# Attention scores as one-pass products of high and low parts, with the maxima subtracted in a product of their own

## The chip, the cores and the metric

One NeuronCore of a Trainium2 chip runs the whole program. The metric is the device time of one execution, in microseconds (us). Engines are named as in the profile: PE (TensorE) with its weight loads PEld, DVE (VectorE), ACT (ScalarE), POOL (GpSimd), SP (SyncE, which issues the DMAs).

## The reference

Input x is 8 batches of 512 tokens by 256 numbers, f32. Four layers follow, each on a layer norm of x, with its result added to x:

- layer 0, causal attention: 16 heads of 16 numbers, queries and keys rotated (RoPE), scores divided by 4, masked above the diagonal, softmax, values, output weights;
- layers 1 and 3, gated attention: a sigmoid gate picks the 256 best of the 512 tokens; among them attention with 16 heads of 16 numbers, without mask; the result is multiplied by the gate and put back at the tokens' places;
- layer 2, biased attention: 16 heads of 64 numbers, with a table of relative biases added to the scores.

```python
scores = jnp.einsum('bhnd,bhmd->bhnm', Q, K) / jnp.sqrt(jnp.asarray(d_k, x.dtype))
scores = jnp.where(causal, scores, -jnp.inf)
attn = jax.nn.softmax(scores, axis=-1)
out = jnp.einsum('bhnm,bhmd->bhnd', attn, V)
```

## The kernel before

All data stays in SBUF. The program is a list of steps (`Step(kind, s, l, n, q)`: kind, batch, layer, number), `c_*` for the causal layers, `f_*` for the gated and `b_*` for the biased ones. A batch's layers depend on each other, so layers of several batches run interleaved: from the third batch on, the order is a cycle in which the biased layer of one batch is mixed with the last gated layer of the batch before it and the causal and first gated layer of the next batch. `in_order` makes one order of all steps from a table of turns (`PLACE`), a table of durations (`WORK`) and dependencies; every engine runs its part of that order, and semaphores counted by `Plan` connect them. PSUM has eight banks, which `in_order` gives out too. Where PE would wait for over 1 us by that plan, L1341 has it transpose the identity.

**A causal layer.** `c_ln` and `c_xt` normalise and transpose x. `c_q` and `c_k` (n = 0, 1; 8 heads each) project; DVE turns pairs (L1159, L1160) and POOL finishes the rotation (L999, L1001). A group of 32 rows then holds two heads, 16 rows each. `c_hq` (ACT, L1051, L1052) makes two copies of the queries: in each, one head's rows are scaled by 1/4 and the other's are zero. `c_hk` (DVE, L1165, L1166) makes two copies of the keys, with the other head's rows zero and one of them minus one.

`c_p1` computes scores with queries as weights, four heads side by side in the four groups of 32 rows of PE, each into its own bank (L1379). DVE takes the row maxima (L1176, for a gated layer L1251) into `mcol`. `c_m` transposes `mcol` on PE (L1389), and DVE adds the maxima into the free rows of the queries (L1184), where they meet the key row of minus one. `c_p2` computes the scores again, transposed and with the maxima subtracted (L1399); ACT takes the exponential (L1057); POOL zeroes what lies above the diagonal (L1007). `c_va` and `c_vb` multiply by the values (L1413), beside which a column of ones gives the sums; DVE divides (L1195 to L1206). `c_y` applies the output weights. The steps come in three parts, since key tile t meets only queries from tile t on: products are 128 to 512 columns wide.

**A gated layer** does the same with 256 tokens (two tiles, products of 256 columns): `f_q` (ACT, L1062) and `f_k` (DVE, L1240) make the copies right out of PSUM, `f_p1` is L1469, `f_m` L1479, `f_p2` L1488. It also gathers and spreads tokens by products whose operands are F32R (a float that PE takes in one pass), split into a high and a low part (L1033, L993, L1072, L1282).

Every other product has f32 operands; each shows as two records in the trace.

## Time and profile before

| | us |
|---|---|
| median of 3 runs | 2102.8 (2101.93 to 2104.2) |
| profiled execution, its time | 2105.06 |
| its span | 2103.3 |
| busy: PE | 2029.9 (97%) |
| PEld | 1243.3 (59%) |
| DVE | 1467.4 (70%) |
| ACT | 1110.2 (53%) |
| POOL | 600.8 (29%) |

The span is the time from the first to the last instruction. Busy time of PE counts its matmul records with modelled ends, records that overlap once. The DMAs move 98.56 MB, 47 GB/s in the mean.

### The profile page before, as it was taken

Reading aid. Unit: us, or ns where it says so; the run is one execution under the profiler, and the core shown is the slowest. Engines: PE = TensorE matmul, PEld = TensorE weight load, DVE = VectorE, ACT = ScalarE, POOL = GpSimd, SP = SyncE. Lnnn points to the kernel's source line nnn. Section 1 sums busy time; section 2 is a strip of 40 time slices with the busy share of each in tenths; the row PEclk is TensorE's granted clock in tenths of the full one; section 3 lists DMA queues with packets and bytes.
Section 4 is the critical chain, followed back from the end, with each engine's and each line's share of the span. In section 5 each row is a group of like instructions: output and inputs, shape, how many; then the busy total and the mean of one; then the engine's idle time right before and its main releaser. Section 6 shows DMA issues by size and latency. Waiting matters only on the chain.

```text
span 2103.3 us, 38722 instructions
## 1 busy us (share of the span) xinstructions
PE 2029.9 (97%) x14644; PEld 1243.3 (59%) x14644; DVE 1467.4 (70%) x4578; ACT 1110.2 (53%) x2497; POOL 600.8 (29%) x817
## 2 busy tenths in 40 slices
PE   7889999999999999999999999999999999999997
PEld 4456556655665555765566645666456654666565
DVE  8887654777757766678767687576875777866435
ACT  1444664746537474464734646365563656535642
POOL 4212132243222342233411423124231243212220
PEclk9999999999999999999999999999999999999998
DMA  3001121121111110111101111012100121111200
GB/s 143 2 1 41 43 76 58 50 81 34 44 41 57 57 44 26 48 67 48 42 21 58 58 47 44 18 59 71 46 31 27 51 73 49 44 34 51 76 3 11
DMA packets 29047, 98.56 MB, mean 47 GB/s; under 512 B 2880, under 2 KB 11200, under 8 KB 28736
## 3 DMA queue, kind: packets, MB, share of 16 engines
q1 hardware_dynamic: 28864, 96.09, 13.6%
q8 instruction: 118, 1.93, 0.4%
q14 instruction: 65, 0.53, 0.1%
HBM read 91.89 MB, written 4.19 MB: 46 GB/s over the span
## 4 chain that ended last, share of the span: by engine, by line
PE 85%; DVE 7%; ACT 6%; issue 1%; POOL 0%; DMA 0%; SPq 0%; DVEq 0%; ACTq 0%; POOLq 0%
PE ps L861 26%; PE ps L1532 11%; PE ps L1550 10%; PE ps L1322 9%; PE ps L1540 9%; PE ps L1379 4%; PE ps L1488 3%; PE ps L1399 3%; PE ps L1500 3%; PE ps L1469 3%; PE ps L1413 2%; ACT PTc L1057 2%; ACT PT L1097 2%; DVE ps L1176 2%; DVE mcol L1251 1%; ACT probs L1088 1%
## 5 line engine op out<-in xcount | busy, mean ns | idle before, releaser
L1015 POOL TENSOR_SCALAR probs<-probs,rtotal 128x512 f32<-128x512 f32 x512 | 344.9, 693 | 871.8 <-DVE rtotal L1277 871.3
L1088 ACT ACTIVATE probs<-probs,peak 128x512 f32<-128x512 f32 x512 | 365.0, 714 | 220.9 <-DVE peak L1273 220.9
L1268 DVE CUSTOM_DVE_ANT_0 probs<-ps,band 128x512 f32<-128x512 f32 x512 | 332.6, 687 | 107.8 <-PE ps L1532 106.4
L1097 ACT ACTIVATE PT<-ps 128x512 f32<-128x512 f32 x512 | 263.1, 619 | 78.1 <-PE ps L1540 77.9
L1176 DVE CUSTOM_DVE_ANT_0 ps<-ps,later 128x128 f32<-128x128 f32 (+3 forms) x512 | 233.3, 525 | 40.9 <-PE ps L1379 40.0
L1540 PEld LDWEIGHTS ps<-ident,probs 128*128 128x128 f32 x2048 | 223.3, 141 | 52.0 <-issue 43.3
L1532 PE MATMUL ps<-KT,QT 64*128 64x512 f32 x1024 | 252.4, 611 | 0.0
L1540 PE MATMUL ps<-ident,probs 128*128 128x128 f32 x2048 | 248.3, 275 | 0.1
L1550 PE MATMUL ps<-PT,Vb 128*64 128x512 f32 x1024 | 235.9, 600 | 0.1
L861 PE MATMUL ps<-xnT,wb 128*128 128x512 f32 x512 | 233.0, 598 | 1.3 <-ACT PT L1097 0.7
L1057 ACT ACTIVATE PTc<-ps 128x384 f32<-128x384 f32 (+1 forms) x384 | 167.7, 542 | 64.8 <-PE ps L1399 64.7
L1251 DVE TENSOR_REDUCE mcol<-ps 128x2 f32<-128x512 f32 x256 | 157.3, 683 | 14.8 <-PE ps L1469 14.0
L1068 ACT ACTIVATE PTf<-ps 128x512 f32<-128x512 f32 x256 | 131.7, 604 | 63.0 <-PE ps L1488 62.6
L861 PEld LDWEIGHTS ps<-xnT,wb 128*128 128x128 f32 x512 | 92.9, 190 | 102.0 <-issue 96.8
L1532 PEld LDWEIGHTS ps<-KT,QT 64*128 64x128 f32 x1024 | 94.5, 186 | 92.9 <-issue 67.9
L1550 PEld LDWEIGHTS ps<-PT,Vb 128*64 128x64 f32 x1024 | 67.1, 137 | 139.2 <-issue 121.8
L861 PEld LDWEIGHTS ps<-wb,xnT 128*128 128x128 f32 x1024 | 122.6, 192 | 26.5 <-issue 16.7
L1007 POOL TENSOR_SCALAR_AFFINE_SELECT PTc<-PTc 128x512 f32<-128x512 f32 x128 | 82.1, 654 | 178.0 <-ACT PTc L1057 177.3
L983 POOL TENSOR_TENSOR rstd<-veps,pow_half 128x2 f32<-128x2 f32 x64 | 47.0, 737 | 280.8 <-DVE veps L1118 280.8
L861 PE MATMUL ps<-wb,xnT 128*128 128x128 f32 x1024 | 125.7, 276 | 0.0
L1322 PE MATMUL ps<-wob,OTb 128*128 128x256 f32 x512 | 114.0, 380 | 0.8 <-DVE OTb L1279 0.8
L1379 PE MATMUL ps<-K,Qz 32*128 32x128 f32 (+3 forms) x1024 | 96.5, 471 | 14.8 <-ACT PTc L1057 4.9
(133 smaller groups left out, 2887.3 us busy)
## 6 DMA issues: line engine op xcount, KB each, us to landing
band<-in_band SPq DMA_DIRECT2D x64, 896.0 KB, 4.6
wb<-in_w_b SPq DMA_DIRECT2D x64, 384.0 KB, 3.0
x<-in_x SPq DMA_DIRECT2D x16, 256.0 KB, 2.9
out<-x SPq DMA_DIRECT2D x16, 256.0 KB, 2.2
wob<-in_wo_b SPq DMA_DIRECT2D x1, 1024.0 KB, 8.7
wqk<-in_wqk_a SPq DMA_DIRECT2D x1, 512.0 KB, 6.2
cos_t<-in_cos SPq DMA_DIRECT2D x1, 256.0 KB, 5.4
sin_t<-in_sin SPq DMA_DIRECT2D x1, 256.0 KB, 6.5
```

The lines of the kernel that those rows point to most:

```text
L861: last = nc.tensor.matmul(o, w, r, start=(i == 0), stop=(i == len(pairs) - 1))
L1015: last = g.tensor_scalar(unit, unit, rtotal[:, r % 8, e:e + 1], 1.0, ALU.mult, ALU.mult)
L1057: a.activation(pt_c(m, q)[:, h], bank(now, name)[:, 0:w], ACT.Exp).then_inc(act_read, 1)
L1088: last = a.activation(unit, unit, ACT.Exp, bias=peak[:, r % 8, e:e + 1], accum_out=total[:, r % 8, e:e + 1])
L1097: a.activation(PT[:, k % 2, e, :, tile_of(q)], bank(now, name).rearrange("p (k n) -> p k n", k=NT), ACT.Copy).then_inc(act_read, 1)
L1176: last = v.tensor_tensor_reduce(out=scores, in0=scores, in1=later[:, NT * P - w:NT * P], scale=1.0, scalar=-3e38, op0=ALU.add, op1=ALU.max ...
L1268: v.tensor_tensor_reduce(out=probs[:, r % ROWS_HELD, e, :], in0=bank(now, name), in1=band[:, k % 2, e, lo:lo + T], scale=1.0, scalar=-3e38 ...
L1322: last = te.matmul(o[:, j * D:(j + 1) * D], w, r, start=(k == 0 and j == 0), stop=(k == count - 1 and j == 1))
L1379: last = te.matmul(o[h][:, at_:at_ + w], m.Qz[group(h), c, e, tile_of(t)], m.K1[group(h), c, e, 0:w], start=True, stop=True)
L1532: full(te.matmul(bank(now, name), QT2[half(e), k % 2, tile_of(q)], KT2[half(e), k % 2, :], start=True, stop=True), now, name)
L1540: last = te.transpose(bank(now, name)[:, tile_of(t)], probs[:, r % ROWS_HELD, e, tile_of(t)], ident[:])
L1550: last = te.matmul(o[half(e), :], Vb[:, k % 3, q, half(e)], PT[:, k % 2, e, q, :], start=(q == 0), stop=(q == NT - 1))
```

## The change

Queries and keys of the causal and gated layers are stored as F32R. A head's 16 numbers are copied to all 32 rows of a group, and X holds the high part of the queries in 16 rows and the rest (the low part) in the other 16. HI holds the high part of the keys in both halves, LO the rest in both. X by HI plus X by LO is then the full product. The first score product is these two, the second these two and a third one, in which a selecting weight `sel` (0 and -1) picks the high and low part of the maxima from M. The factor 1/4 moves into the exponential.

New steps: `c_dq`, `c_dk` (DVE: two shuffles each that copy one head's rows to both halves), `c_rq`, `f_rq` (ACT: X = plus or minus the copy, rounded), `c_xq`, `f_xq` (DVE: X = copy in the low half + X), `c_hk`, `f_hk` (ACT: HI; POOL: LO = copy - HI), `c_hm`, `f_hm` (DVE: high and low part of the maxima, in small pieces). `c_m` and `f_m` are read out by ACT instead of DVE. `f_q` and `f_k` become two shuffles each from PSUM. The values lie closer together (17 columns a head instead of 32), the work memory of the layers is laid out anew, and both tables `PLACE` and `WORK` are new, so the order of all steps is another.

```diff
     for i in range(2):
-        out += [(c("q", i), [c("xt")], []), (c("k", i), [c("xt")], []), (c("hq", i), [c("q", i)], []),
-                (c("hk", i), [c("k", i)], [])]
+        out += [(c("q", i), [c("xt")], []), (c("k", i), [c("xt")], []), (c("dq", i), [c("q", i)], []),
+                (c("rq", i), [c("dq", i)], []), (c("xq", i), [c("rq", i)], []), (c("dk", i), [c("k", i)], []),
+                (c("hk", i), [c("dk", i)], [])]
...
+                        if kind in ("c_hk", "f_hk"):
+                            for e in range(2):
+                                pool.wait_ge(high_k_done, plan.after("high_k", now, now) - 1 + e)
...
+                                last = g.tensor_tensor(low, both, high, ALU.subtract)
+                            last.then_inc(halves_k_done, 1)
...
+                            act.wait_ge(pairs_q_done, plan.after("pairs_q", Step("c_dq", s, l, n), now))
+                            for e in range(2):
+                                last = a.activation(m.X[:, n, e], m.Dq[:, n, e], ACT.Copy, scale=sides[:, 0:1])
+                            last.then_inc(signed_done, 1)
+                        if kind in ("c_m", "f_m"):
+                            parts = m.M[n][:] if kind == "c_m" else m.M[:, n]
+                            a.activation(parts, bank(now) if kind == "c_m" else bank(now)[:, 0:CAP],
                                          ACT.Copy).then_inc(act_read, 1)
...
                         if kind == "c_p2":
                             _, w = c_p2_parts(q)
+                            if n == 0 and q == 0:
+                                act.wait_ge(halves_q_done, plan.after("halves_q", Step("c_xq", s, l, 1), now))
...
+                                a.activation(pt_c(m, q)[:, h], bank(now, name)[:, 0:w], ACT.Exp,
+                                             scale=float(DH) ** -0.5).then_inc(act_read, 1)
...
+                            for e in range(2):
+                                last = v.stream_shuffle(pairs[:, n, e], turned, [DH * e + r % DH for r in range(32)])
+                            last.then_inc(done, 1)
+                        if kind in ("c_xq", "f_xq"):
...
+                                last = v.scalar_tensor_tensor(out=parts, in0=both, scalar=sides[:, 1:2], in1=parts,
+                                                              op0=ALU.mult, op1=ALU.add)
...
+                            v.tensor_copy(split[:, :, :, 0:2], top[:, :, :, 4:6]).then_inc(high_m_done, 1)
+                            dve.wait_ge(high_m_done, plan.after("high_m", now, now))
+                            v.tensor_tensor(split[:, :, :, 2:4], top[:, :, :, 4:6], split[:, :, :, 0:2],
+                                            ALU.subtract).then_inc(halves_m_done, 1)
...
                             for t, at_, w in parts:
-                                for h in range(4):
-                                    last = te.matmul(o[h][:, at_:at_ + w], m.Qz[group(h), c, e, tile_of(t)],
-                                                     m.K1[group(h), c, e, 0:w], start=True, stop=True)
...
+                                for some in (m.LO, m.HI):
+                                    for h in range(4):
+                                        last = te.matmul(o[h][:, at_:at_ + w], m.X[group(h), c, e, tile_of(t)],
+                                                         some[group(h), c, e, 0:w], start=(some is m.LO), stop=(some is m.HI))
...
                             for t, at_, w in parts:
-                                for h in range(4):
-                                    last = te.matmul(o[h][:, at_:at_ + w], m.K1[group(h), c, e, tile_of(t)],
-                                                     m.Qz[group(h), c, e, t * P:T], start=True, stop=True)
...
+                                for i in range(3):
+                                    for h in range(4):
+                                        one = sel[group(h), e:e + 1].to_broadcast([32, P])
+                                        w_ = (m.LO[group(h), c, e, tile_of(t)], m.HI[group(h), c, e, tile_of(t)], one)[i]
+                                        r_ = m.M[c][group(h), t * P:T] if i == 2 else m.X[group(h), c, e, t * P:T]
+                                        last = te.matmul(o[h][:, at_:at_ + w], w_, r_, start=(i == 0), stop=(i == 2))
```

## Rows read from the trace of the kernel before

**Rows 1.** Busy time by stretch: us, then PE, PEld, DVE, ACT, POOL, clock, DMA.

```profile
0.00:160.00 160.00, 132.40 (x1125) 74.94 (x1125) 132.83 (x422) 59.47 (x125) 49.78 (x69) 0.96 0.13 48
160.00:2045.00 1885.00, 1854.82 (x13145) 1135.33 (x13142) 1301.55 (x4075) 1038.89 (x2350) 547.75 (x745) 1.00 0.14 48
2045.00:2103.30 58.30, 42.65 (x380) 33.04 (x378) 33.06 (x81) 11.87 (x23) 3.31 (x3) 0.91 0.03 10
```

**Rows 2.** The same of one period, the second of five alike.

```profile
840.00:1093.00 253.00, 248.87 (x1806) 151.09 (x1806) 182.35 (x572) 138.90 (x312) 74.54 (x100) 1.00 0.14 47
```

**Rows 3.** Records of one line by stretch: L1379 (first row), then L1469; PE, PEld.

```profile
0.00:160.00 160.00, 25.65 (x256) 10.59 (x256) 0.96 0.13 48
...
0.00:160.00 160.00, 4.30 (x64) 3.09 (x64) 0.96 0.13 48
2045.00:2103.00 58.00, 4.30 (x64) 3.09 (x64) 0.91 0.03 10
```

**Rows 4.** Groups by line: busy us, mean ns, idle before and releasers.

```profile
L1469 PE MATMUL ps<-K1f,Qzf 32*128 32x256 f32 x1024 | 72.5, 398 | 9.9 <-DVE mcol L1251 3.0 <-DVE peak L1268 1.8 <-ACT Qzf L1062 1.7
```

**Rows 5.** Timeline of PE, last gated layer: start, us, line, form, count.

```profile
2071.72 2.01 PE L1469 MATMUL ps<-K1f,Qzf 32*128 32x256 f32 x32 [0.59 <-ACT Qzf L1062]
2075.51 1.15 PE L1469 MATMUL ps<-K1f,Qzf 32*128 32x256 f32 x16 [1.78 <-DVE mcol L1251]
```

**Rows 6.** Timeline of PE, causal layers (the first row holds 128 and 256 columns).

```profile
477.67 0.94 PE L1379 MATMUL ps<-K,Qz 32*128 32x128 f32 x16
...
50.97 0.93 PE L1379 MATMUL ps<-K,Qz 32*128 32x384 f32 x8 [0.86 <-DVE mcol L1176]
52.30 1.14 PE L1379 MATMUL ps<-K,Qz 32*128 32x512 f32 x8 [0.41 <-ACT PTc L1057]
```

**Rows 7.** Timeline of PE, one-pass products; two of another tile lie between.

```profile
2098.15 0.40 PE L1322 MATMUL ps<-of_hi,spread_t 128*128 128x256 f32 x2
...
2098.63 0.40 PE L1322 MATMUL ps<-of_hi,spread_t 128*128 128x256 f32 x2
```

**Rows 8.** Groups by line of DVE.

```profile
L1159 DVE STREAM_SHUFFLE Qz<-ps 128x512 f32<-128x512 f32 x16 | 11.8, 735 | 0.0
L1206 DVE STREAM_TRANSPOSE Qz<-Qz 128x512 f32<-128x512 f32 x16 | 11.4, 711 | 0.5
L1165 DVE TENSOR_SCALAR K<-K,sides 128x512 f32<-128x512 f32 x16 | 11.3, 708 | 0.4 <-POOL K L1001 0.4
L1166 DVE TENSOR_SCALAR K<-K,sides 128x512 f32<-128x512 f32 x16 | 15.3, 953 | 0.0
L1184 DVE SCALAR_TENSOR_TENSOR Qz<-ps,sides,Qz 128x512 f32<-128x512 f32 x32 | 22.4, 741 | 0.9 <-PE ps L1389 0.9
L1184 DVE SCALAR_TENSOR_TENSOR Qzf<-ps,sides,Qzf 128x256 f32<-128x256 f32 x64 | 28.0, 478 | 23.1 <-PE ps L1479 23.1
L1240 DVE TENSOR_SCALAR K1f<-ps,sides 128x512 f32<-128x512 f32 x32 | 24.4, 804 | 11.4 <-PE ps L861 11.4
L1273 DVE TENSOR_SCALAR peak<-peak 128x2 f32<-128x2 f32 x256 | 49.9, 195 | 8.9
```

**Rows 9.** Groups by line of ACT and POOL.

```profile
L1072 ACT ACTIVATE of_hi<-ps 128x512 fp32r<-128x512 f32 x16 | 9.6, 597 | 56.6 <-PE ps L1322 56.6
L993 POOL TENSOR_TENSOR xn_lo<-xn,xn_hi 128x512 fp32r<-128x512 f32 x32 | 40.1, 1275 | 62.1 <-ACT xn_hi L1033 62.1
```

**Rows 10.** One line's instructions: duration ns min/median/max.

```profile
L1201 DVE TENSOR_TENSOR scaledf<-turnedf,rsums x64: 291/292/749, 154.9 to 2093.3; 128x128 f32<-128x128 f32 x64
```

**Rows 11.** Timeline, first score product and last gated layer's queries.

```profile
25.31 1.67 PE L1379 MATMUL ps<-K,Qz 32*128 32x128 f32 x16 [3.95 <-ACT Qz L1052]
...
2070.40 1.26 ACT L1062 ACTIVATE Qzf<-ps,sides 128x512 f32<-128x512 f32 x2 [5.82 <-PE ps L861]
```

**Rows 12.** Timeline of PE, products of one column; four lie between the two.

```profile
111.11 0.16 PE L861 MATMUL ps<-ones,tie 128*128 128x1 bf16 x1
...
111.23 0.16 PE L861 MATMUL ps<-ones,tie 128*128 128x1 bf16 x1
```

718 lines of the change are left out of this document (407 added, 311 removed).

## The prediction

> **What bounds the kernel now.** I read the busy time by stretch first, then one cycle, then the timeline at both ends.
> TensorE (PE) is busy for 1854.8 of the 1885 us between 160 and 2045 us [rows 1], at the full clock: this is the bound. That part is a pattern of 253.1 us, repeated; in one period PE is idle for 4.1 of 253 us, while VectorE (DVE) is busy for 182 us, 72% [rows 2]. A microsecond of PE work taken out there shortens the span, as long as DVE keeps up.
> The ends are different. In the first 160 us PE is idle for 27.6 us and DVE is busy for 132.8 us, 83%: a chain through all engines, with DVE nearest to the bound. In the last 58.3 us PE is idle for 15.7 us [rows 1].
> The changed products are a small part of PE's time. Two of the eight causal layers have their first score products in the first 160 us (256 of 1024 records); one of the sixteen gated layers has its own there, one in the last 58 us (64 each of 1024) [rows 3]. So 6 causal and 14 gated layers lie where PE is the bound.
>
> **What a score product costs now.** An f32 product is two records (1024 records for 512 products of L1469) [rows 4]. Four heads sit in four groups of 32 rows and run side by side; I call four such records a batch. 32 records of 256 columns take 2.01 us and 16 take 1.15 [rows 5]: 0.86 us for four batches, 0.215 each. The step with two batches of 128 and two of 256 columns takes 0.94 [rows 6], 0.21 less than four of 256, so 128 columns cost 0.1075 a batch. 512 against 384 columns is 1.14 against 0.93 for two batches [rows 6], again 0.105 per 128 columns. So a batch takes 0.43, 0.3225, 0.215 and 0.1075 us for 512, 384, 256 and 128 columns, in proportion, weights included.
>
> **What one costs after.** The operands become one-pass floats (F32R): queries X (high part in 16 rows, low part in the other 16), keys HI and LO. The first product needs two records (X by LO, X by HI), as many as now. The second needs three: the third subtracts the maxima. The trace has one-pass products of 256 columns: four start within 0.48 us, 0.12 each [rows 7]. That is 0.0125 more than half of 0.215, so something besides the columns counts, most likely the load of the weights. I take 0.12 for 256 columns and half of today's price for 384 and 512 (0.161, 0.215). For 128 columns nothing is shown: at least 0.054 (half of today's), at most 0.215 (four passes, twice today's); I take 0.12, the nearest one-pass row.
> Per four heads of a causal layer, each width counted once: now 1.075 times 2 = 2.15 us in either product; after, 0.616 times 2 = 1.23 in the first and times 3 = 1.85 in the second. It saves 0.92 and 0.30, times 4 per layer 4.88 us. Gated, two tiles of 256: 0.86 now, 4 x 0.12 = 0.48 and 6 x 0.12 = 0.72 after; 0.52 times 4 = 2.08 us per layer. All layers: 8 x 4.88 + 16 x 2.08 = 72.3 us. Where PE is the bound: 6 x 4.88 + 14 x 2.08 = 58.4 us.
> The Trainium skill ("TensorE: Matmul & The Clock Gate", section "LDWEIGHTS (loading the stationary operand)") gives columns / 1.2 GHz for a weight load, whatever the rows: 107 ns for 128 columns. By it the load would set the pace of narrow products and speak against splitting them: 128-column batches gain nothing and the third one is pure loss. With 0.107 for both 128 and 256 columns the 72.3 would be 84.8. The trace fits it as far as it goes: f32 at 128 columns shows 0.1075, which two passes explain as well.
> The four transposes of the maxima per step stay (two in a gated layer).
>
> **What the other engines get.** DVE loses, per causal layer, L1165 and L1166 (2 x (0.708 + 0.953)) and four of L1184 at 0.741: 6.3 us. It gains eight shuffles, at 0.735 as from PSUM (the transposes of L1206, SBUF to SBUF, take 0.711, so the source matters little), four X updates with two SBUF inputs at 0.741, and four tiny splits of the maxima at 0.195: 9.6. Net +3.3. Per gated layer it loses 2 x 0.804 + 4 x 0.478 = 3.5 and gains 4 x 0.735 + 2 x 0.741 + 4 x 0.195 = 5.2, net +1.7 [rows 8]. In all +54 us on 1467, +6.7 us in a cycle.
> ScalarE (ACT) gains, per causal layer, four high copies (0.6) and two copies of the maxima (0.6); its four scaled copies stay: +3.6. Gated: +2.4 at most. GpSimd (POOL) gains four, or two, subtractions of 1.275 us: 82 us in all [rows 9]. Both have room in a cycle (139 and 75 of 253 us [rows 2]); other work of PE, the biased layer, hides them. DMAs don't change; the queues are passed by no new transfer.
> New waits: ACT, at the first exponentials of a causal layer, waits for the second half of X; behind it stand copies for the biased layer. The work memory overlaps more closely too, so some steps get a fixed order. I price these in the idle time.
> DVE seems to be held up now and then already: L1201, which reads two SBUF tensors, takes 0.292 us in the median and 0.749 at most [rows 10]. The Trainium skill ("SBUF — State Buffer", section "SBUF: two separate sides") has an exclusive lock on a port pair: a DVE operation with two SBUF inputs and a GpSimd one block each other for a whole instruction. The 64 new X updates and 48 subtractions of maxima are of that kind. By it, with POOL busy for a third of the time, a third of the 112 would wait for half a POOL instruction (0.64), 24 us of DVE time and one point of its share, which the bounds of the idle time hold.
>
> **Idle time in the middle.** It can stay at 4.1 us in a cycle (bound below), or follow DVE's share (bound above): 72% with 1.6% idle in a cycle, 83% with 17% in the first stretch. After the change DVE has 189 of some 245 us, 77%. The first stretch is one chain with little to fill it in, the middle has the biased layer, so I stay near the lower end: 1 us more a cycle, over 7.4 cycles 7 us.
>
> **The ends.** At the start PE waits for ACT's scaled copy of the queries until 25.31 [rows 11]. The way from the rotated query to the product is two ACT copies, 1.26 us if they are as those of L1062 [rows 11]; it becomes two shuffles (1.47), two copies and two updates (1.48), 4.2. The keys' way becomes two shuffles, a copy and two POOL subtractions, 4.6 instead of the 1.7 of L1165 and L1166 [rows 8, 9]. That is 3 us until the first product, and 3 again in the first gated layer, whose queries and keys go the same ways. Together +6. Faster products don't give this back while DVE works on the maxima. Bounds: -14 (all of PE's savings there count), +16 (DVE's extra 10 us come on top of the 6).
> At the end the same 3 before the first product of the last gated layer (at 2071.72 [rows 5]), and -0.5 for earlier maxima and a shorter way through them: +2.5. The exponentials on ACT set the pace there, not PE.
>
> **Sum.** -58.4 + 7 + 6 + 2.5 = -42.9 us. The profiled execution took 2105.06 us (span 2103.3 and 1.8 around it), 2.3 above the median of 2102.8. So 2062, or 2060 as a median.
>
> **Rivals.**
> A, everything counts: the new order hides the ends and the idle time stays. -72.3, 2030; if narrow batches cost half of today's, another 20 less (160 of 128 columns by 0.066, 800 of 256 by 0.0125), 2010. For it: five like cycles with 4 us idle show how well the order can fit. Against it: 83% DVE in the first 160 us. 0.20.
> B, 128 columns take four passes: 160 batches (64 in the first, 96 in the second products) times 0.095, 15 us more: 2075. No row for or against. 0.14.
> C, DVE becomes the bound, on the slower side. Place: the waits of PE for banks of score tiles that DVE reads the maxima from, in the middle. If the idle time follows DVE's share to 9%, half way between the two stretches, it is 23 us a cycle, 19 more, 141 in all instead of 7: 2194. At half that growth, which I hold for more likely, it is 70 instead of 7: 2123, the time I give it. It decides from 7 us more a cycle on, where the 42.9 are used up. Against it: in the middle DVE's work is independent of PE's next step most of the time. 0.09, a part of which ends near no change.
> D, records can't be issued this fast. A batch of four in 0.107 us is 27 ns a record; the fastest stream shown is five records in 0.12 us [rows 12], 24 ns, but with weights of another type. At 50 ns a batch takes 0.2; 960 narrow batches times 0.08, and 6 for those of 384 columns, are 83 more: 2143. Break-even near 41 ns. 0.06.
> My forecast, between 2040 and 2074: 0.51.
>
> **How the numbers follow.** 2060 is the likeliest. 2018 to 2094 takes in A's 2030 but not its outer end, and B; it leaves out C and D. A difference of 0.2% (4 us) is what can be told from none. Slower takes most of C and D, 0.10; within 0.2% 0.04; faster 0.86.
>
> **What would show it.** One-pass batches of four heads 0.12 us apart, 0.16 and 0.215 for the wide ones; if those of 128 columns are 0.2 apart, it is B, if all are near 0.2, D. A cycle of about 245 us with some 5 us of PE idle; 250 or more, with PE waiting for DVE, is C. The first score product after 28 us, biased layers starting some 6 us later. DVE near 1520 us, POOL near 680. I am wrong if PE's busy time falls by less than 60 us or if its idle time, 73 us now, grows by more than 30.

## The result and the profile after

The changed kernel takes 2115.5 us (median; 2111.4 to 2120.6), the kernel before in the same job 2103.2. The ratio is 1.0056, 95% interval 1.0037 to 1.0075: it is slower by half a per cent, where 2060 was forecast. The profiled execution took 2120.6 us, its span is 2117.8. It is the slowest of the five and 5 us above their median; the clock (below) is most of the difference.

Busy time by stretch of the changed kernel; columns as in [rows 1], and behind them one of its periods, as in [rows 2]:

```profile
0.00:160.00 160.00, 121.11 (x1045) 80.84 (x1049) 133.04 (x447) 51.82 (x108) 56.65 (x69) 0.79 0.13 48
160.00:2045.00 1885.00, 1810.76 (x14154) 1135.66 (x14148) 1377.37 (x4288) 1097.29 (x2476) 629.61 (x804) 0.99 0.15 48
2045.00:2117.80 72.80, 56.35 (x503) 47.40 (x501) 39.22 (x100) 14.55 (x28) 6.53 (x6) 0.90 0.05 15
...
1110.00:1363.20 253.20, 242.21 (x1935) 152.43 (x1934) 193.30 (x604) 145.37 (x326) 86.41 (x108) 0.99 0.14 47
```

The period has hardly changed: 253.2 us in this one, 253.5 in the mean of six, where the kernel before has 252.7. TensorE's busy time in it fell from 248.9 to 242.2, and its idle time rose from 4.1 to 11.0. DVE does 193.3 us of work in place of 182.3; 189 had been forecast.

Where the time went by place. As marks I take the first product with the output weights (`wob`) in the first and in the last biased layer, that is near the layer's end. In the kernel after they start as follows (timeline of PE: start, us, line, form, count); in the kernel before they start at 338.20 and 2032.66 us:

```profile
350.81 0.63 PE L1440 MATMUL ps<-wob,OTb 128*128 128x256 f32 x2
...
2044.87 0.59 PE L1440 MATMUL ps<-wob,OTb 128*128 128x256 f32 x2
```

So the start, up to that first mark, costs 12.6 us. What lies between the marks gives back 0.4 (1694.1 for 1694.5): six periods are longer by 0.8 each, and the shorter stretch behind them takes 173.3 in place of 178.3. What follows 2044.87 takes 72.9 in place of 70.6, 2.3 more. The sum is the 14.5 us between the spans.

The products themselves came out as forecast. The last gated layer once more, as in [rows 5], now by batches of four records:

```profile
2085.02 0.29 PE L1593 MATMUL ps<-gHI,gX 32*128 32x256 f32 x4
2085.14 0.29 PE L1593 MATMUL ps<-gLO,gX 32*128 32x256 f32 x4
2085.25 0.29 PE L1593 MATMUL ps<-gHI,gX 32*128 32x256 f32 x4
2085.37 0.29 PE L1593 MATMUL ps<-gLO,gX 32*128 32x256 f32 x4
...
2088.55 0.45 PE L1593 MATMUL ps<-gHI,gX 32*128 32x256 f32 x4
2088.77 0.45 PE L1593 MATMUL ps<-gLO,gX 32*128 32x256 f32 x4
```

At the full clock a batch starts 0.12 us behind the last, as in [rows 7]; the last two rows show 0.22 for the same batch at half clock. At the full clock, within a run of such batches, the next one mostly comes 0.058 to 0.116 us behind one of 128 columns, 0.12 behind 256, 0.17 behind 384 and 0.22 to 0.23 behind 512. Behind the first batch of a run the trace has some 0.07 more (0.13 to 0.17 for 128 columns).

What PE waits for between 160 and 2045 us, in its four largest groups (us in total, times, longest):

```profile
PE ps L1498 <- DVE X L1279: 12.8, 12, 1.9
PE ps L943 <- DVE above L1344: 8.4, 6, 1.4
PE ps L1522 <- DVE peaks L1295: 7.9, 6, 1.3
PE ps L1593 <- DVE peaks L1369: 7.0, 12, 0.9
```

In the kernel before PE's largest wait there is for ACT's exponentials (6.2 us), and the largest for DVE is 3.7. The first row is the wait for the new update of the queries; the two with `peaks` are waits for banks from which DVE has yet to take the maxima. One such place, DVE's timeline first, then GpSimd's, then PE's (start, us, line, form, count, and in brackets the idle time before it and its releaser):

```profile
968.89 0.76 DVE L1272 STREAM_SHUFFLE Dq<-Xf 128x512 f32<-128x512 f32 x1
969.54 3.35 DVE L1279 SCALAR_TENSOR_TENSOR X<-Dq,sides,X 128x512 fp32r<-128x512 f32 x2
...
968.18 2.50 POOL L1087 TENSOR_TENSOR LO<-LOf,HI 128x512 fp32r<-128x512 f32 x2
970.63 1.71 POOL L1077 TENSOR_TENSOR HIf<-HIf,sin_t 128x512 f32<-128x512 f32 x1
...
972.95 0.33 PE L1498 MATMUL ps<-LO,X 32*128 32x128 f32 x4 [1.93 <-DVE X L1279]
```

and the same two instructions 32 us later, with no GpSimd work beside them:

```profile
1001.73 1.41 DVE L1279 SCALAR_TENSOR_TENSOR X<-Dq,sides,X 128x512 fp32r<-128x512 f32 x2
```

3.35 against 1.41 us, 1.94 more, and PE is idle for 1.93 at that place. The first update starts 0.1 us into the second GpSimd subtraction and ends 0.5 us behind it, the second waits out the rotation's product; the shuffle above, which reads one SBUF tensor, keeps its 0.76 beside the same GpSimd instruction. The groups (ns min/median/max):

```profile
L1279 DVE SCALAR_TENSOR_TENSOR X<-Dq,sides,X x32: 742/1096/1840, 22.7 to 1764.0; 128x512 fp32r<-128x512 f32 x32
L1279 DVE SCALAR_TENSOR_TENSOR gX<-gDq,sides,gX x32: 743/1060/1822, 143.0 to 2084.0; 128x512 fp32r<-128x512 f32 x32
L1272 DVE STREAM_SHUFFLE Dq<-Xf x32: 735/750/779, 18.8 to 1730.6; 128x512 f32<-128x512 f32 x32
```

The eight updates of a period take 9.6 us; at 0.74 they would take 5.9. Behind the idle time the clock goes down too (window rows as above; the seventh figure is the granted clock):

```profile
966.00:973.70 7.70, 5.78 (x29) 2.52 (x28) 7.03 (x13) 2.58 (x5) 7.54 (x6) 1.00 0.00 0
973.70:977.20 3.50, 3.50 (x14) 2.14 (x16) 2.93 (x17) 1.19 (x2) 0.33 (x1) 0.53 0.02 5
```

PE had been idle for 1.9 us, then ran 3.4 us at 1.2 in place of 2.4 GHz. There are eight such drops between 160 and 2045 us, and none in the kernel before, whose longest gap there is 1.03 us. Four come behind this wait for X (1.9 us), four behind the wait for the maxima at L1522 (1.3 us); each of the two waits comes six times at the same length, and two times without a drop. A third wait, of 1.4 us, comes six times and has none behind it. So a gap of this length can cost a drop and need not. A period with one drop lasts 253.3 us, one with two 254.9: 1.6 us each, 13 in all. The number differs between executions: the mean clock is 0.974 in the profiled one and 0.979 in the two fastest, which take 9 us less. By my estimate (0.005 of 2115 us, lost at half speed) that is 21 us less at half clock and some 10 us of time, so most of the difference between executions is the clock, and the median execution likely has fewer than eight drops.

### The profile page after: what moved, and what is told of

Read it like the earlier page. It is cut to its first block, busy times and chain, and to the rows that moved or that the text cites. A ratio compares the mean times of both kernels' runs of the same rounds, so it can differ in the third digit from the quotient of the medians.

```text
span 2117.8 us, 41412 instructions
## 1 busy us (share of the span) xinstructions
PE 1988.2 (94%) x15696; PEld 1263.9 (60%) x15696; DVE 1549.6 (73%) x4835; ACT 1163.7 (55%) x2610; POOL 692.8 (33%) x879
## 4 chain that ended last, share of the span: by engine, by line
PE 70%; DVE 18%; ACT 6%; POOL 3%; issue 2%; DMA 0%; SPq 0%; DVEq 0%; POOLq 0%
PE ps L943 17%; PE ps L1678 10%; PE ps L1660 10%; PE ps L1440 9%; PE ps L1668 7%; DVE ps L1295 3%; ACT PTc L1166 3%; PE ps L1522 3%; PE ps L1536 3%; PE ps L1627 3%; PE ps L1498 2%; DVE peaks L1369 2%; DVE probs L1386 2%; PE ps L1615 2%; PE ps L1593 2%
## 5 line engine op out<-in xcount | busy, mean ns | idle before, releaser
L1102 POOL TENSOR_SCALAR probs<-probs,rtotal 128x512 f32<-128x512 f32 x512 | 352.3, 708 | 549.5 <-DVE rtotal L1395 549.2
L1202 ACT ACTIVATE PT<-ps 128x512 f32<-128x512 f32 x512 | 264.5, 610 | 71.2 <-PE ps L1668 70.6
L1295 DVE CUSTOM_DVE_ANT_0 ps<-ps,later 128x512 f32<-128x512 f32 (+3 forms) x512 | 232.9, 525 | 32.1 <-PE ps L1498 31.9
L1668 PE MATMUL ps<-ident,probs 128*128 128x128 f32 x2048 | 254.3, 277 | 0.5
L1166 ACT ACTIVATE PTc<-ps 128x384 f32<-128x384 f32 (+1 forms) x384 | 167.1, 545 | 42.4 <-PE ps L1522 41.5
L1369 DVE TENSOR_REDUCE peaks<-ps 128x2 f32<-128x512 f32 x256 | 157.3, 682 | 14.0 <-PE ps L1593 13.9
L943 PE MATMUL ps<-wb,xnT 128*128 128x128 f32 x1024 | 132.3, 285 | 0.0
L1440 PEld LDWEIGHTS ps<-wob,OTb 128*128 128x128 f32 x512 | 96.4, 190 | 12.6
```

The costliest lines, as they stand in the source:

```text
L943: last = nc.tensor.matmul(o, w, r, start=(i == 0), stop=(i == len(pairs) - 1))
L1102: last = g.tensor_scalar(unit, unit, rtotal[:, r % 8, e:e + 1], 1.0, ALU.mult, ALU.mult)
L1166: a.activation(pt_c(m, q)[:, h], bank(now, name)[:, 0:w], ACT.Exp, scale=float(DH) ** -0.5).then_inc(act_read, 1)
L1202: a.activation(PT[:, k % 2, e, :, tile_of(q)], bank(now, name).rearrange("p (k n) -> p k n", k=NT), ACT.Copy).then_inc(act_read, 1)
L1295: last = v.tensor_tensor_reduce(out=scores, in0=scores, in1=later[:, NT * P - w:NT * P], scale=1.0, scalar=-3e38, op0=ALU.add, op1=ALU.max ...
L1369: v.tensor_reduce(places[:, h:h + 1].rearrange("p h t -> p (h t)"), bank(now, name).rearrange("p (t n) -> p t n", t=NS), AXIS.X, ALU.max). ...
```

## The experiments

The runs came in five jobs, in which the kernel before has medians of 2103.8 to 2105.4 us. Each ratio is against the kernel before of its own job; differences between jobs are taken from the ratios (0.01 is 21 us) and are good to 3 to 5 us, by the intervals of the two ratios. Periods are read from the profiled execution alone; a mean of six is taken between the marks of the first seven biased layers. Line numbers are those of each run's own kernel.

**TensorE's part alone.** Before, with one-pass products in the number that the change has. Low parts are left out, the products of each kind being repeated instead.

```
-    last = te.matmul(o[h][...], m.Qz[...], m.K1[...], start=True, stop=True)      # f32
+    for again in range(2):                                                        # 3 in c_p2, f_p2
+        for h in range(4): last = te.matmul(o[h][...], m.QR[...], m.KR[...], ...)  # F32R
```

> The kernel before with its own order and its own side work; only the score products are one-pass records, as many as in the change (each product issued twice in the first, three times in the second score product, each time over the same bank). Left out: the low parts, so the scores are rounded. Theory S (the side work and the longer ways eat what PE saves): the whole gain of PE shows here, 2040 to 2055 us, a cycle of about 244 us. Theory K (one-pass products leave PE too idle and its clock falls to half, mostly in the first 160 us): the middle gains, but the first 160 us show 50 us or more at the half clock and the time is 2060 to 2075. If PE's time is worth nothing in this schedule at all: 2095 or more.

2072.2 us, ratio 0.9852 (0.9837 to 0.9868): 32 us, not 58 to 72. A period of it:

```profile
1079.80:1328.00 248.20, 240.88 (x1935) 151.59 (x1934) 181.99 (x572) 138.59 (x312) 74.27 (x100) 1.00 0.15 48
```

PE works 8.0 us less in a period ([rows 2] has 248.9 in 253.0), and the period is 4.8 shorter; the rest, 3.2 us, has become idle time, with DVE's work unchanged. The time lies in theory K's range, but only 24 us before 160 us are at half clock, where K wanted 50 or more. Theory S had 2040 to 2055 and a period of 244, so it doesn't hold in full either: a part of the gain is missing without any new side work.

**The rest of the change alone.** The changed kernel, each score product one f32 product of X by HI (the low part of the keys and the product with the maxima are left out of the scores, all side work is kept).

```
-    for some in (m.LO, m.HI):  ... te.matmul(o[h][...], m.X[...], some[...], start=(some is m.LO), ...)
+    for some in (m.HI,):       ... te.matmul(o[h][...], m.X[...].bitcast(F32), some[...].bitcast(F32), start=True, ...)
```

> The changed kernel, its order and side work unchanged, but each score product is one f32 product of X by HI (two records, as before the change), so PE has the cost of the kernel before. Left out: LO, the maxima in the second product. Theory S (PE is no longer the bound): it costs little, 2110 to 2135 us. If PE's saving still counts in full in the changed kernel: 2175. Theory K: the clock stays up in the first 160 us, and the start is shorter than in the changed kernel by some 8 us although PE has more work.

2156.5 us, ratio 1.0257 (1.0234 to 1.0280): the side work and the new order cost 52 us when TensorE saves nothing. Theory S had 2110 to 2135, and 2175 stood for a saving that counts in full; the changed kernel is 42 us below this run, so TensorE's saving is worth 42 us in it.

```profile
1125.70:1385.60 259.90, 250.90 (x1807) 151.61 (x1806) 194.63 (x604) 145.97 (x326) 86.65 (x108) 0.99 0.14 46
```

6.6 us in a full period (6.3 in the mean of six), and 12 until the first mark (350.2): the whole loss of the start is in this part.

**Is it the new order?** The changed kernel under the turn table of before (steps that it lacks placed at those they split from).

```
-    PLACE = { ... }   # the new table
+    PLACE = { ... }   # that of the kernel before
```

> The changed kernel under the table of turns of the kernel before: the common steps have their old turns, a new step the turn of the step it stems from (c_dq, c_rq, c_xq that of c_hq; c_dk, c_hk that of c_hk; c_hm that of c_m; f_rq, f_xq that of f_q; f_hk that of f_k; f_hm that of f_m). Theory O (the new order is what lost the gain): 2050 to 2085 us. Theory S: 2110 to 2140, since the old turns know nothing of the side work.

2364.6 us, ratio 1.1241 (1.1224 to 1.1259), a period of 286.7; both theories had expected less than 2140. So the old table isn't the better one for this work: the new order hides most of what the side work would cost in the old one. The planner saw the waits too: PE transposes the identity 1230 times in this run and 272 times in the changed kernel. What the new order costs by itself, with the side work of before, no run shows.

**Is it the clock at the start?** Dummy one-pass batches in the causal layers of the first two sequences, two in the first score product (shown) and one in the second.

```
+    for _ in range(2 if s < 2 else 0):
+        for h in range(4): te.matmul(o[h][...], m.X[...], m.HI[...], start=True, stop=True)
```

> The changed kernel, but in the causal layers of the first two batches PE issues more one-pass records over the same banks, four instead of two in the first and four instead of three in the second product, which is what the f32 products cost. The result is the same. Theory K: the time at the half clock in the first 160 us falls from 75 us to under 30, and the start is shorter by 5 to 12 us: 2103 to 2110 us. Theory S: PE waits there for DVE anyway, 2114 to 2120.

2122.4 us, ratio 1.0093 (1.0073 to 1.0113). The time at half clock before 160 us fell from 68 to 34 us, and the first mark came at 350.9, for 350.8 in the changed kernel. PE has more work there and a faster clock, and the start is the same to 0.1 us: it waits for other engines, unless the two cancel. The whole is 7 to 8 us slower than the changed kernel's median, but this profiled execution has eight drops between 160 and 2045 us and takes 2121.0, like the changed kernel's profiled one.

**What is TensorE's time still worth?** As the first run, each product once.

```
-    for again in range(2):
+    for again in range(1):
```

> The kernel before with each score product one one-pass product (no second or third pass over the bank; the low parts of queries and keys are left out), its order and side work unchanged. Against the run with two and three passes (2072.2) it takes away 32 batches of four records at 0.12 or less in every cycle of the scores of one causal and two gated layers, some 5 to 6 us of TensorE a cycle by the 0.118 measured for a batch behind 256 columns. Theory A (TensorE is still the bound in before's side work, what it saves is mostly given back): 3 to 5 us a cycle less, 2035 to 2050. Theory B (with its order kept, the kernel is already at the limit of VectorE and the waits, so that TensorE's time no longer counts): under 1.5 us a cycle, 2062 to 2072.

2049.3 us, ratio 0.9738 (0.9724 to 0.9753), 24 us less again. PE has some 11 us less to do in a period (I had written 5 to 6), and the period falls from 248.3 to 245.2, the mean of six: less than a third of TensorE's time is paid back. A part goes to the clock: between 160 and 2045 us 48 us are at half clock, 17 in the first run.

**Taking the update of the queries out** (and with it their low part); PE, and ACT before the first exponentials of a causal layer, wait for ACT's rounded copy.

```
-    if kind in ("c_xq", "f_xq"): ... v.scalar_tensor_tensor(out=parts, in0=both, ...)
-    at_least(pe, halves_q_done, ...)
+    at_least(pe, signed_done, ...)
```

> The changed kernel without the second step on the queries (VectorE's multiply-add of 0.72 us, 8 in a cycle = 5.8 us, about 56 in all), TensorE waits for ScalarE's rounded copy in its place; the low part of the queries is left out, order and everything else kept. Theory V (VectorE's added work, and its place at the end of the queries' chain, makes TensorE wait): the waits for X (12.8 us in the middle, 12 of them) go and some of the others shorten, 3 to 5 us a cycle, 2075 to 2095. Theory O (the new order, found for costs of its own, is what takes the time; waits only change their names): within 1 us a cycle, 2108 to 2118. Theory K (the keys' chain over ScalarE and GpSimd is as late as the queries'): the same as O here, and the next run moves.

2081.6 us, ratio 0.9886 (0.9869 to 0.9902): 36 us below the changed kernel and some 5 a period, as theory V had it. The first mark comes at 343.2, 7.6 us sooner.

**The update moved to ACT and GpSimd**, same result:

```
+    a.activation(m.Dq[...], m.Dq[...], ACT.Copy, scale=sides[:, 1:2]).then_inc(signed_done, 1)
-    last = v.scalar_tensor_tensor(out=parts, in0=both, scalar=sides[:, 1:2], in1=parts, ...)
+    last = g.tensor_tensor(parts, both, parts, ALU.add)
```

> The changed kernel with the same result, the second step on the queries moved off VectorE: ScalarE scales the pairs (0.65 us, 8 more in a cycle) and GpSimd adds them (1.3 us, 8 in a cycle). VectorE has 5.8 us a cycle less, the queries' chain is some 2.5 us longer from the shuffle to the last write where it has no queue to stand in. Theory V by occupancy (VectorE's time counts wherever it falls): 2085 to 2105. Theory V by latency (only the end of the queries' chain counts): slower than the changed kernel by up to 2.5 us at each of 24 causal and gated layers, 2120 to 2160. Theory O: 2110 to 2125.

2213.3 us, ratio 1.0513 (1.0492 to 1.0534). DVE is busy for 186.6 us a period instead of 193.3, and the period is 266. PE now waits for GpSimd:

```profile
PE ps L1591 <- POOL gX L1084: 45.1, 12, 5.6
PE ps L1496 <- POOL X L1084: 28.5, 6, 4.8
```

It is slower than the 2120 to 2160 expected of the longer way alone, and 113 us of its middle are at half clock. How late X is counts, wherever it is made.

**GpSimd's low part of the keys left out**; PE takes the rounded keys twice.

```
-    if kind in ("c_hk", "f_hk"): ... last = g.tensor_tensor(low, both, high, ALU.subtract)
-    for some in (m.LO, m.HI):
+    for some in (m.HI, m.HI):
```

> The changed kernel without GpSimd's low part of the keys (1.4 us each, 8 in a cycle); TensorE takes the rounded keys twice, so the number of its products is kept; order and the rest kept. The low part of the keys is left out. The keys' chain is 2.8 us shorter. Theory K: 3 us a cycle or more and an earlier first score product, under 2100. Theories V and O: within 1 us a cycle in the middle, 2105 to 2118; at the start the first score product may come up to 2.8 us earlier.

2095.1 us, ratio 0.9953 (0.9938 to 0.9968): 22 us below the changed kernel. In part it isn't the keys that come earlier, but the updates of the queries that are no longer held up:

```profile
L1270 DVE SCALAR_TENSOR_TENSOR X<-Dq,sides,X x32: 737/745/1832, 22.5 to 1741.7; 128x512 fp32r<-128x512 f32 x32
```

The median is 745 ns, against 1096 with GpSimd's subtractions beside it.

**Handing on by half.** Same work, order and result; signals for each of the two halves.

```
+    dve.wait_ge(signed_done, plan.after("signed", ..., now) - 1 + e)      # inside the loop over e
-    at_least(pe, halves_q_done, plan.after("halves_q", Step("c_xq", s, l, c), now))
+    at_least(pe, halves_q_done, plan.after("halves_q", Step("c_xq", s, l, c), now) - 1 + e)   # keys alike
```

> The changed kernel, same work, same order, same result, but its two preparation chains are handed on by half (head e=0 or 1) and not by pair: VectorE's second step on half 0 starts when ScalarE has rounded half 0, and TensorE's first score product of a pair waits for half 0 alone (of the keys' low part too; in gated layers ScalarE also starts behind the first shuffle). The queries' chain to the first product is some 1.2 to 2 us shorter, the keys' 1.4. Theory L (the time from projection to score product is paid nearly whole, since the order is fixed and holds no more work between: without the queries' second step, 1.44 us shorter, a cycle took 249 in place of 254): 4 to 6 us a cycle less, 2070 to 2092. Theory V (what counts is how long VectorE is occupied): no more than 1 us a cycle, 2108 to 2118.

2104.1 us, ratio 0.9992 (0.9980 to 1.0005): 13 us of the loss come back. That is between the theories: 2.7 us a period, where L wanted 4 to 6 and V no more than 1. Not all of it is latency: the eight updates of a period take 8.9 us in place of 9.6, and the middle of this profiled execution (2097.5 us, of the faster ones) has three drops, not eight. The first mark comes at 342.4, 8.4 us sooner.

**The update kept, but with PE not waiting for it** (ACT still does, before the first exponentials of a causal layer).

```
-    last = v.scalar_tensor_tensor(out=parts, in0=both, ...)      # PE: halves_q_done
+    last = v.scalar_tensor_tensor(out=both, in0=both, ...)       # PE: signed_done
```

> The changed kernel with the queries' second step still run by VectorE at its place in the order, but into a place that no score product reads: TensorE waits for ScalarE's rounded copy, as in the run without that step. The low part of the queries is left out of the scores. Theory L (its latency counts, VectorE's 5.8 us a cycle don't): 2080 to 2088, as without it (2081.6). Theory V: most of the 35 us comes back, 2100 to 2117.

2105.3 us, ratio 1.0005 (0.9995 to 1.0015). The ratio was 0.9886 without the update, is 1.0005 with it, and 1.0056 with PE's wait too: some 25 us go with DVE's occupied time (ACT's remaining wait is in them), 11 with PE's wait. Theory L, which I favoured by then, falls as the main cause.

**Both cuts together.**

```
-    if kind in ("c_xq", "f_xq"): ...
-    if kind in ("c_hk", "f_hk"): ... g.tensor_tensor(low, both, high, ALU.subtract)
```

> The changed kernel without the queries' second step and without GpSimd's low part of the keys, products and order kept (both low parts are left out). Theory L: the two savings don't overlap where one chain waits for the other, so more than either alone: a cycle of 244 to 247, 2050 to 2070. If the two cuts together give no more than the queries' alone (2078 to 2084), the rest of the loss is the order's or that of the other edits.

2078.4 us, ratio 0.9875 (0.9861 to 0.9890). That is 2 us below the first cut alone, which can't be told from none: the keys' subtractions cost mostly through the queries' updates. It is still some 5 above the first experiment, with the shuffles, the splits and the new order left.

**The keys' low part on DVE**, on top of the version by halves, same result.

```
-    pool.wait_ge(high_k_done, ...);  last = g.tensor_tensor(low, both, high, ALU.subtract)
+    dve.wait_ge(high_k_done, ...);   v.tensor_tensor(low, both, high, ALU.subtract)
```

> As the version that hands on by halves, and the low part of the keys is subtracted by VectorE (some 0.7 us each) and not by GpSimd (1.4 us): the keys' chain is 1.4 us shorter still, and VectorE has 8 x 0.7 = 5.6 us a cycle more to do. Same result. Theory L: the same as by halves or up to 2 us a cycle faster, 2060 to 2090. Theory V: 3 to 5 us a cycle slower than by halves.

2148.9 us, ratio 1.0211 (1.0179 to 1.0243), 45 us above the version by halves, though the keys' way is shorter.

```profile
DVE gLO L1280 <- ACT gHI L1149: 10.2, 13, 0.8
...
L1280 DVE TENSOR_TENSOR LO<-LOf,HI x32: 678/693/1751, 28.1 to 1778.0; 128x512 fp32r<-128x512 f32 x32
L1280 DVE TENSOR_TENSOR gLO<-gLOf,gHI x32: 683/692/693, 138.1 to 2108.9; 128x512 fp32r<-128x512 f32 x32
```

8 x 0.69 us a period and a wait at the head of DVE's queue, in which it stands still for what is behind it; the longest periods go from 252.0 to 259.4, more than the 3 to 5 us that theory V wanted.

**DVE's time by itself.** The kernel before, and seven idle shuffles of 256 columns behind the keys of every causal pair and gated layer, 28 a period.

```
+    for again in range(7):
+        if spent[0]: dve.wait_ge(spare_done, spent[0])
+        v.stream_shuffle(spare[:], cos_t[:, 0:256], [r ^ 1 for r in range(32)]).then_inc(spare_done, 1)
```

> The kernel before with idle work on VectorE, and nothing else: behind the preparation of the keys of every causal pair and of every gated layer seven shuffles of 256 columns (some 0.4 us each) into a place that nobody reads, 28 in a cycle, 11 to 12 us, what the change added there (182.3 to 193.3 us). No wait and no order is changed, and a shuffle is not held up by GpSimd. Theory S (before has slack: VectorE at 72% can take it): under 2 us a cycle, up to 2120. Theory V (in a fixed order VectorE's time at this place is nearly all on TensorE's path, as the run with the low part of the keys on VectorE showed with 45 us for 6): 6 to 11 us a cycle, 2150 to 2190.

2187.2 us, ratio 1.0392 (1.0376 to 1.0407), 82.5 us more. Its window row and one of its groups:

```profile
1145.60:1410.80 265.20, 253.77 (x1807) 153.45 (x1806) 194.24 (x628) 139.15 (x312) 74.84 (x100) 0.98 0.13 45
...
L1174 DVE STREAM_SHUFFLE spare<-cos_t x112: 432/436/446, 23.4 to 1798.9; 128x256 f32<-128x256 f32 x112
```

This experiment shows that DVE had little time to spare at this place. 28 x 0.436 = 12.2 us of work on an engine that is 72% busy, with no new wait between engines and no change of order, make the period 11.0 us longer (263.7 against 252.7, means of six): 0.9 us for each microsecond of DVE. (Each shuffle waits for the one before it, so seven take 3.31 us from start to end, for 3.06 of work.) In the period shown PE's idle time is 11.4 us in place of 4.1, and its busy time is up by 4.7 with the same products; it holds 10.2 us at half clock, as much as three drops, and at 1.6 us each they are that. So 0.6 of the 0.9 are waits, the rest is the clock. It is the price in an order that wasn't made for this work. In the changed kernel's order, made for its side work, the second experiment has 12 us more of DVE in a period (194.6 for 182.3) and a period 6.3 longer: 0.5 for one, with what ACT and GpSimd add in it.

**The same with two SBUF operands.**

```
-    v.stream_shuffle(spare[:], cos_t[:, 0:256], ...)
+    v.tensor_tensor(spare[:], cos_t[:, 0:256], sin_t[:, 0:256], ALU.mult)
```

> As the run before this, but the seven instructions at each place are products of two SBUF tensors of 256 columns (some 0.3 to 0.35 us each alone). Theory P: where GpSimd is busy each waits for it in addition, and GpSimd for it, so that they cost more per nominal microsecond than the shuffles do; in total near or above the shuffles in spite of a nominal time that is a quarter less. Theory V': three quarters of what the shuffles cost.

2210.1 us, ratio 1.0503 (1.0484 to 1.0522), 23 us more than the shuffles.

```profile
L1174 DVE TENSOR_TENSOR spare<-cos_t,sin_t x112: 417/425/1498, 23.9 to 1812.0; 128x256 f32<-128x256 f32 x112
L1255 DVE TENSOR_TENSOR spare<-cos_t,sin_t x112: 414/424/808, 137.3 to 2174.1; 128x256 f32<-128x256 f32 x112
```

Alone such an instruction takes 0.42 us, the shuffle's 0.44; the quarter less that I expected isn't there. But up to 1.50 beside GpSimd, which the shuffle never shows: 29 of the 224 take over 0.5 us, and all together they take 114.4 us for the shuffles' 97.9.

**Fewer turns.** The changed kernel, the two updates of a step as one instruction of 1024 columns; same work, order and result.

```
-    for e in range(2): ... v.scalar_tensor_tensor(out=m.X[:, n, e], in0=m.Dq[:, n, e], ...)      # 128x512
+    v.scalar_tensor_tensor(out=parts, in0=both, ...)      # m.X[:, n] and m.Dq[:, n], both e: 128x1024
```

> The changed kernel with the queries' second step as one instruction of 1024 columns in place of two of 512; the same work, order and result. In the trace of the changed kernel these instructions take 0.745 us where GpSimd is idle and 1.0 to 1.8 where it runs beside them: each of the two waits for a GpSimd instruction. In a cycle the eight take 9.6 us instead of 5.9. Theory P (the exclusive turn with GpSimd is what makes VectorE's work dearer and later): one instruction waits once; the four take 7.5 to 8 us a cycle, and the cycle gets 1 to 2 us shorter, 2100 to 2110. Theory V' (only nominal time of VectorE counts): unchanged, 2112 to 2120.

2094.6 us, ratio 0.9951 (0.9934 to 0.9967): 22 us below the changed kernel from this alone, and faster than the kernel before.

```profile
L1280 DVE SCALAR_TENSOR_TENSOR X<-Dq,sides,X x16: 1276/1746/2373, 22.5 to 1742.8; 128x1024 fp32r<-128x1024 f32 x16
L1280 DVE SCALAR_TENSOR_TENSOR gX<-gDq,sides,gX x16: 1265/1285/1546, 140.9 to 2060.3; 128x1024 fp32r<-128x1024 f32 x16
...
1097.80:1347.60 249.80, 240.45 (x1935) 151.01 (x1934) 191.35 (x600) 145.08 (x326) 87.07 (x108) 1.00 0.14 48
```

DVE's busy time falls by 1.9 us a period, the period by 3.5. Nearly half of the difference is the clock: this period has no drop. A drop costs 1.6, and four in place of eight lie between 160 and 2045 us. The updates themselves take 6.3 us a period in place of 9.3 (time covered); 0.5 of these 3.0 aren't GpSimd's doing, since alone the wide one takes 1.28 us and the two narrow ones 1.41.

**Shorter turns.** By halves, GpSimd's rotation and subtraction in instructions of 256 columns.

```
-    g.tensor_tensor(low, both, high, ALU.subtract)
+    for part in (slice(0, 256), slice(256, 512)):
+        last = g.tensor_tensor(low[:, part], both[:, part], high[:, part], ALU.subtract)
```

> The version that hands on by halves, with GpSimd's rotation and low part of the keys cut into instructions of 256 columns (same work and result; each GpSimd instruction 0.65 in place of 1.27 us). Theory P: a VectorE instruction with two SBUF operands waits at most half as long, the queries' second step in the first causal pair takes 1.2 to 1.4 us in place of 1.7, 1 to 2 us a cycle less than by halves: 2090 to 2100. Against it: GpSimd's own chain grows by its fixed cost per instruction, and more instructions mean more turns lost. Theory V': 2100 to 2108, or slower.

2094.4 us, ratio 0.9956 (0.9939 to 0.9973), 8 us below the version by halves.

```profile
L1287 DVE SCALAR_TENSOR_TENSOR X<-Dq,sides,X x32: 725/754/1302, 22.5 to 1741.8; 128x512 fp32r<-128x512 f32 x32
```

The update's median falls from 1093 ns in the version by halves to 754, the longest from 1.8 to 1.3 us.

**All together**, without and with the shorter turns; same result as the changed kernel.

```
+    v.scalar_tensor_tensor(...)  128x1024;  a.activation(m.X[:, n] ..., m.Dq[:, n] ...)  128x1024
+    keys handed on by half; in the second kernel GpSimd by 256 columns
```

> A version meant to beat both, same result and order as the changed kernel: the queries' second step as one instruction of 1024 columns, ScalarE's rounding of the queries too, and the keys handed on by half as in the version that hands on by halves. Its wide step alone gave 23 us, the halves alone 13; the keys' part of the halves is perhaps half of the latter. If the savings add: 2082 to 2092, a cycle near 249. If TensorE's waits are elsewhere by now (the exponentials, 11 us, and the gate's comparisons, 8 us, wait last in the wide one): no better than the wide one, 2092 to 2097.

> The same with GpSimd's rotation and low part in instructions of 256 columns. On top of the halves the split gave 10 us. Where VectorE has one wide instruction there are fewer turns to wait for: 0 to 6 us less than the kernel without the split, 2076 to 2092.

2092.7 us, ratio 0.9942 (0.9923 to 0.9962), and 2091.5, ratio 0.9943 (0.9931 to 0.9955). They beat the kernel before by 0.6% and the changed one by 1.1%, but the gains don't add: 22 for the wide update, 13 and 8 for the others, 24 together, which can't be told from the wide update alone. The wide update, the hand-on and the short turns get back the same microseconds. Behind them stand other waits (first kernel, 160 to 1900 us); in the changed kernel the first was 3.2 us, the second the same and the third 7.0:

```profile
PE ps L1523 <- ACT PTc L1166: 11.1, 18, 1.3
PE ps L944 <- DVE above L1345: 8.4, 6, 1.4
PE ps L1594 <- DVE peaks L1370: 5.7, 6, 0.9
```

## Why the prediction was wrong

**TensorE's part: right.** The batch prices were right (0.12 forecast, 0.12 measured for 256 columns), and so was their sum. Between 160 and 2045 us PE is busy for 44.1 us less; with the 13 us that the drops of the clock add to it, 57 us were saved at the full clock, against 58.4 in the sum. Rivals B (four passes at 128 columns) and D (issue rate) are refuted by the narrow batches, 0.058 to 0.116 us apart within a run. The other price that the prediction names, 0.107 for both widths, isn't borne out either: 256 columns take 0.118.

**The step that failed: "1 us more a cycle" of idle time.** It was 6.9 by the window rows, and 44 us over the middle instead of 7. I read PE's 4 us of idle time as a sign that DVE, 72% busy, had 70 us a period to spare. But every engine runs a fixed order. DVE's free time lies mostly where it waits for PE, not where its work is needed, and what is added ahead of a product that PE has next in its queue is handed to PE in good part: 0.9 us for one in the order of before, 0.5 in the new one. Nor did "a microsecond of PE work taken out there shortens the span" hold: TensorE's part alone gave 4.8 for 8.0 us in a period. PE's idle time in a period puts the two together: 4.1 us before, 7.3 with TensorE's part alone, 9.0 with the rest of the change alone, 11.0 with both. So nearly half of the growth needs no side work: waits that the f32 products had covered show once the products are shorter. By this and by the idle load, before the change other engines, DVE above all, bounded the period nearly as closely as PE, though only PE showed it.

**The side work by its terms.** DVE's 6.7 us a period were 11.0. Of the missing 4.3 us, 3.7 are the updates that take turns with GpSimd (9.6 for 5.9). I had weighed this lock with 24 us of DVE time in all, for a third of the 112 instructions that stand in its way; the 64 updates alone took 28 us more than 0.744 each, 39 of them over 0.8. The Trainium skill ("SBUF — State Buffer", section "SBUF: two separate sides") says that the two engines lock each other out for a whole instruction, and the trace agrees: 1.75 us in place of 0.74 beside a GpSimd instruction of 1.27. The kernel before had more of it than the one row I showed: L1166, one of the copies of the keys, takes 0.53 us at least and 1.49 at most, which its mean of 0.953 in [rows 8] hides. The error was not its size but to let "the bounds of the idle time hold" it: they priced it at nothing on the path, and it fell in the very place that PE waited for. All side work with the new order costs 6.3 us a period and 12 at the start (second experiment), against 1 and 6 in the sum.

**The clock** was no term at all. Eight times a gap of 1.3 to 1.9 us in a dense stretch was followed by 3.4 us at 1.2 GHz: 13 us of the 51 that are missing in the middle of the profiled execution, less in the median one. The other 37 are the idle time.

**The ends.** The last one came out (+2.3 for +2.5). The start is +12.6 for +6. The first score product comes 6.5 us later (31.78 for 25.31), not 3: the first updates of the queries take 1.84 and 1.75 us there beside GpSimd, and the keys' first shuffle starts only behind them, at 26.1. By the profile the product itself waits last for the second pair's updates, 28.61 to 31.73, which run beside GpSimd's subtractions for the keys (these end at 31.18):

```profile
31.78 0.33 PE L1498 MATMUL ps<-LO,X 32*128 32x128 f32 x4 [1.18 <-DVE X L1279]
```

Of the bounds, -14 to +16, the upper one was the nearer, as DVE's 83% in that stretch said. The clock isn't the cause, as far as the run with dummy batches can tell. The two ways that X and the keys take are most of it: the first mark comes 7.6 us sooner without the update, 4.9 without GpSimd's subtraction, 9.8 without both, and 8.4 sooner when both ways are only handed on by half. What carries the other 3 us stays open.

**The rival that won was C**, in its mechanism (PE waits for DVE in the middle), with 2123 for a measured 2115. It had a chance of 0.09. Its place is half of it: the waits for `peaks`, 7.9 and 7.0 us, are for banks from which DVE takes the maxima, as C says, but the largest, 12.8 us, is for X, which C doesn't name. That its time comes so near is in part luck: it has 63 us more idle time in the middle than the forecast and nothing else, and the runs have 37 of idle time, 13 of the clock and 7 at the start. Its deciding point, 7 us more idle time a period, is what came (6.9), and it was held for unlikely for a reason that no row bore out: that "DVE's work is independent of PE's next step most of the time". The forecast's own test told this at once: the period is over 250 and the idle time is up by 56. PE's busy time, the third sign, fell by 41.7 us, not 60, though the prices of the products are right; the likely reason is more time at half clock (68 us for 14 before 160 us, and the eight drops).

The chain from update to clock is shown at one place by its rows, and the run with the wide update shows it in the sum; how the 36 us for the update divide (25 and 11) holds for this order only. What the new order and the closer work memory cost apart from the side work is not shown. Not tried: a turn table found for the true durations (the new `WORK` has 0.7 us for the update, which took 1.1 in the median), which might give more than the versions above.

## What to carry to other kernels

In a fixed order an engine at 72% can be nearly as much a bound as one at 98%: before pricing an addition, ask who has its product next in the queue, and don't price it at nothing. An idle load at that place gives the price before anything is rewritten: here 0.9 us for one in an order not made for it, and 0.5 was paid with an order made for the work. A saving on the busiest engine is checked the same way, by a version that has only the saving: here it gave about half of what TensorE's time promised. An instruction of VectorE with two SBUF operands is priced with the GpSimd instruction that can run beside it; make such instructions few and wide, or GpSimd's short, and look at their minimum and median, not their mean. And where work is taken from TensorE, count what the gaps do to its clock.

## What the runs showed of the hardware

- VectorE's update of 512 columns with two SBUF operands takes 0.74 us alone and up to 1.84 beside GpSimd's tensor instructions of 1.27, which in their turn grow to 1.7; a shuffle with one operand stays within 0.72 to 0.79 in the same places. Two instructions of 512 columns back to back can lose a turn each (3.35 us for 1.41); one of 1024 columns takes 1.28 us alone and at most 2.37, a single turn more.
- The next one-pass batch of four 32-row products comes 0.12 us behind one of 256 columns, and 0.058 to 0.116 behind one of 128, within a run of such batches.
- Single drops of the clock of 3.4 us cost 1.6 us each in a stretch where PE is the bound. At the start, where PE waits for others, 34 us less at half clock (with more work for PE) left the time as it was.
- Gaps of 1.3 and 1.9 us at the same place of each period were followed by such a drop in eight of twelve cases, and executions of one kernel differ by 9 us with it.
